# Feed-forward first products in three passes of split operands

## What is computed

```python
def ffn_layer(x, g, bln, W1, b1, W2, b2):
    mu = x.mean(-1, keepdims=True)
    var = ((x - mu) ** 2).mean(-1, keepdims=True)
    xn = (x - mu) / jnp.sqrt(var + 1e-05) * g + bln
    hg = xn @ W1 + b1
    a, gate = jnp.split(hg, 2, -1)
    return a * jax.nn.gelu(gate, approximate=False) @ W2 + b2
for i in range(DEPTH):            # 6 layers
    x = attn_layer(shift_tokens(x), Wqkv[i], q_scale[i], k_scale[i], Wo[i]) + x
    x = ffn_layer(shift_tokens(x), ln_g[i], ln_b[i], W1[i], b1[i], W2[i], b2[i]) + x
```

## Time and profile before

| | us |
|---|---|
| median of 3 runs | 2177.5 |
| lowest and highest run | 2176.08, 2187.78 |
| the profiled execution | 2168.39 |
| its span, first to last instruction | 2166.6 |

### The profile page before, as it was taken

How to read it: one execution, slowest core, us unless ns; L and a number is a source line. 1 busy time by engine, 2 the same in 40 slices (tenths; PEclk the granted TensorE clock), 3 DMA queues, 4 the chain that set the end, 5 groups by cost and what they waited for, 6 DMA issues and landing times.

```text
span 2166.6 us, 88603 instructions
## 1 busy us (share of the span) xinstructions
PE 1976.6 (91%) x37428; PEld 1424.8 (66%) x37428; DVE 1793.1 (83%) x3762; ACT 1633.8 (75%) x3052; POOL 1188.8 (55%) x1449
## 2 busy tenths in 40 slices
PE   6888899987789998999989999999999999899997
PEld 4666664455467776777767776677767777677774
DVE  6788775677789897898879988888888888888994
ACT  4777753365567897888888888888888888788883
POOL 1112110000477776766766768667776767767761
PEclk9999999998899998999999999999999999999999
DMA  5000011100122223232322323223233322333231
GB/s 115 2 2 2 2 31 46 43 1 26 41 64 75 62 76 90 66 81 68 79 77 68 79 66 103 68 59 87 60 90 78 79 68 69 88 76 83 59 79 41
DMA packets 98220, 132.57 MB, mean 61 GB/s; under 512 B 27900, under 2 KB 42882, under 8 KB 97826
## 3 DMA queue, kind: packets, MB, share of 16 engines
q1 hardware_dynamic: 97826, 126.90, 22.5%
HBM read 28.20 MB, written 1.11 MB: 14 GB/s over the span
## 4 chain that ended last, share of the span: by engine, by line
PE 65%; DVE 14%; ACT 9%; issue 8%; POOL 3%; SPq 0%; DMA 0%; DVEq 0%; POOLq 0%; ACTq 0%
PE oo L588 22%; PE pj L588 20%; PE sc L588 9%; PE tr L1011 7%; ACT arena L1886 7%; PE tr L591 4%; POOL arena L2316 2%; DVE arena L1462 1%; DVE arena L1707 1%; PE oo L591 1%; DVE xn L1294 1%; PE sc L591 1%; DVE arena L1705 1%; DVE arena L1736 1%; DVE arena L1713 1%
## 5 line engine op out<-in xcount | busy, mean ns | idle before, releaser
L1886 ACT ACTIVATE arena<-tr 128x512 f32<-128x512 f32 (+2 forms) x874 | 455.9, 568 | 135.4 <-PE tr L1011 67.7
L2298 POOL TENSOR_TENSOR arena<-arena 128x1024 f32<-128x1024 f32 x192 | 456.4, 2377 | 57.7 <-DVE arena L1707 54.1
L1886 ACT ACTIVATE arena<-arena 128x16 f32<-128x16 f32 (+6 forms) x808 | 356.0, 456 | 112.2 <-DVE arena L1462 74.1
L1886 ACT ACTIVATE arena<-pj 128x512 f32<-128x512 f32 x576 | 333.7, 597 | 86.1 <-PE pj L588 77.0
L2316 POOL TENSOR_TENSOR arena<-arena 128x1024 f32<-128x1024 f32 x192 | 365.5, 1904 | 27.5
L1705 DVE TENSOR_TENSOR arena<-pj,rtab 128x512 f32<-128x512 f32 x384 | 262.7, 684 | 59.1 <-ACT arena L1886 58.8
L1707 DVE TENSOR_TENSOR arena<-pj,rtab 128x512 f32<-128x512 f32 x384 | 261.4, 681 | 0.0
L1713 DVE TENSOR_REDUCE arena<-arena 128x8 f32<-128x512 f32 x384 | 251.8, 676 | 0.0
L588 PE MATMUL oo<-slab,arena 64*32 64x64 f32 (+1 forms) x12416 | 232.9, 229 | 10.2 <-issue 9.7
L2265 POOL TENSOR_SCALAR rstd<-mv 128x4 f32<-128x4 f32 x40 | 11.4, 284 | 400.6 <-DVE mv L1288 400.4
L591 PE MATMUL tr<-ident,arena 128*128 128x128 f32 x1346 | 207.0, 281 | 26.1 <-ACT arena L1886 12.1
(11 more groups left out here) (288 smaller groups left out, 3883.3 us busy)
## 6 DMA issues: line engine op xcount, KB each, us to landing
slab<-arena SPq DMA_DIRECT2D x576, 128.0 KB
slab<-arena SPq DMA_DIRECT2D x336, 64.0 KB
wqkv<-in_L_ffn_Wqkv SPq DMA_DIRECT2D x18, 512.0 KB, 3.6
arena<-gate_mem SPq DMA_DIRECT2D x24, 256.0 KB, 4.6
wo<-in_L_ffn_Wo SPq DMA_DIRECT2D x6, 512.0 KB, 4.8
w<-in_L_ffn_W SPq DMA_DIRECT2D x6, 341.0 KB
YT<-in_L_attn_x SPq DMA_DIRECT2D x4, 256.0 KB, 3.7
arena<-in_L_ffn_W SPq DMA_DIRECT2D x1, 1024.0 KB
```

The costliest lines, as they stand in the source:

```text
L1886: return nc.scalar.activation(o, i, f, **k)
L2298: p_.tensor_tensor(r_, r_, rb[:, k, :], ALU.add).then_inc(sum_ok, 1)
```

## The change

W1's columns and the normalized rows are split into a rounded copy and a rest, as the projections' operands are, and `ff_up` becomes six passes (three for each half) instead of two full products.

- ACT gains `up_high` (once a layer, in the slot b = 1, t = 3): `w1_hi`, the rounded copy of `w1`, 128 x 682. POOL gains `up_low` in the same slot, behind `add_parts(g, t, 1)`: the rest, written over `w1`.
- ACT gains `hidden_high` (once a batch, at t = 3 behind `ln_finish`): `hB_hi`, 128 x 512. POOL gains `hidden_low`, at t = 0 of the next slot, between `scaled` of the keys and `add_parts`: the rest, written over `hB`.
- TensorE waits for `w1_hi` and its rest at b = 2, t = 0, for `hB_hi` at t = 0, and for the rest of the rows before the third pass of the gate half.
- SP loads W1 in a function of its own (`up_weights`), ahead of the window copies of the slot b = 1, t = 3; it waits for the products of the layer before (`w1_mm`) instead of the second products.
- The gelu output has two buffers instead of three, which makes room for `w1_hi`; in the drain ACT waits for one `ff_gate` more.

```diff
+        w1_lo = nc.alloc_sbuf_tensor_at("w1_lo", [P, 2 * DI], F32R, offset=w1_at)
...
+        hB_hi = nc.alloc_sbuf_tensor_at("hB_hi", [P, S], F32R, offset=xcur_at + 4 * S)
...
+        hB_lo = nc.alloc_sbuf_tensor_at("hB_lo", [P, S], F32R, offset=hT_at)
...
-        ge = a.take(FFC, S)
+        ge = a.take(2, S)
+        w1_hi = nc.alloc_sbuf_tensor_at("w1_hi", [P, 2 * DI], F32R, offset=arena_at + 4 * a.at)
...
+            def up_weights(l):
+                wait(sp, w1_mm, l * B * FFC)
+                sp.dma_start(w1[:, :], ins["L1_ffn_W1"][l:l + 1].rearrange("a k n -> (a k) n")
+                             ).then_inc(ld_w1, 16)
...
+                if s_.later and b == 1 and t == 3:
+                    up_weights(l)
                 if s_.c_:
                     windows(g - 1, (t - 1) % T)
...
             def ff_up(m, k, bank):
-                o, w = CH[k]
-                mm(bank[0:w, 1], w1[:, DI + o:DI + o + w], hB)
-                mm(bank[0:w, 0], w1[:, o:o + w], hB).then_inc(w1_mm, 1)
+                w = CH[k][1]
+                for half, o in ((1, DI + CH[k][0]), (0, CH[k][0])):
+                    mm(bank[0:w, half], w1_hi[:, o:o + w], hB_hi[:, :], stop=False)
+                    mm(bank[0:w, half], w1_lo[:, o:o + w], hB_hi[:, :], start=False, stop=False)
+                    if half:
+                        pe.wait_ge(hb_l, m + 1)
+                    last = mm(bank[0:w, half], w1_hi[:, o:o + w], hB_lo[:, :], start=False)
+                last.then_inc(w1_mm, 1)
...
                     if b == 2 and t == 0:
-                        pe.wait_ge(ld_ff, s_.l2 * 64 + 64)
+                        pe.wait_ge(w1_l, s_.l2 + 1)
+                    if t == 0:
+                        pe.wait_ge(hb_h, m2 + 1)
                     pe.wait_ge(on_ok, g - 1)
                     ff_up(m2, t, oo)
...
+            def up_high(l):
+
+                ac.wait_ge(ld_w1, l * 16 + 16)
+                act(w1_hi[:, :], w1[:, :], ACT.Copy).then_inc(w1_h, 1)
+
+            def hidden_high(m):
+
+                ac.wait_ge(lnb_out, m + 1)
+                act(hB_hi[:, :], hB, ACT.Copy).then_inc(hb_h, 1)
...
                 if t == 3 and m1 is not None:
                     ln_finish(LNB, LNB_BANKS[1], m1, LC(m1, 0), LC(m1, 1), hB)
+                    hidden_high(m1)
...
                 ln_finish(LNB, LAST_NORM[1], MZ, LC(MZ, 0), LC(MZ, 1), hB)
+                hidden_high(MZ)
                 for k in range(FFC):
+                    if k == 2:
+                        ac.wait_ge(ff_ev, MZ * FFC + 1)
                     gelu(MZ, k, LAST_FF[MZ][k])
...
+            def up_low(l):
+
+                gp.wait_ge(w1_h, l + 1)
+                p_.tensor_tensor(w1_lo[:, :], w1[:, :], w1_hi[:, :], ALU.subtract).then_inc(w1_l, 1)
+
+            def hidden_low(m):
+
+                gp.wait_ge(hb_h, m + 1)
+                p_.tensor_tensor(hB_lo[:, :], hB, hB_hi[:, :], ALU.subtract).then_inc(hb_l, 1)
...
                     newton(g - 1, 1)
                     scaled(g - 1, (t - 1) % T, 1)
+                if t == 0 and s_.m2 is not None:
+                    hidden_low(s_.m2)
                 add_parts(g, t, 0)
...
                 add_parts(g, t, 1)
+                if b == 1 and t == 3:
+                    up_low(l)
...
             scaled(TZ, T - 1, 1)
+            hidden_low(MY)
             power(LNB, MZ)
+            hidden_low(MZ)
```

More of the change, by code:

```diff
@@ L160, in build @@
         wo = sb("wo", [P, PAIRS, P])
+        w1_at = here()
         w1 = sb("w1", [P, 2 * DI])
+        w1_lo = nc.alloc_sbuf_tensor_at("w1_lo", [P, 2 * DI], F32R, offset=w1_at)
         w2 = sb("w2", [P, FFC, P])
@@ L170, in build @@
         YT = sb("YT", [P, B * S])
+        xcur_at = here()
         xcur = sb("xcur", [P, 2, S])
+        hB_hi = nc.alloc_sbuf_tensor_at("hB_hi", [P, S], F32R, offset=xcur_at + 4 * S)
         hT_at = here()
         hT = sb("hT", [P, 2, S])
+        hB_lo = nc.alloc_sbuf_tensor_at("hB_lo", [P, S], F32R, offset=hT_at)
         xs_lo = nc.alloc_sbuf_tensor_at("xs_lo", [P, S], F32R, offset=hT_at + 4 * S)
@@ L190, in build @@
         ARENA = 27504
+        arena_at = here()
         arena = sb("arena", [P, ARENA])
@@ L285, in build @@
         oT = a.take(PAIRS, S)
-        ge = a.take(FFC, S)
+        ge = a.take(2, S)
+        w1_hi = nc.alloc_sbuf_tensor_at("w1_hi", [P, 2 * DI], F32R, offset=arena_at + 4 * a.at)
+        a.take(2 * DI)
         fa = a.take(FFC, S)
@@ L346, in build @@
             sem("pt_cp"), sem("o_mm"), sem("o_cp"), sem("wo_mm"), sem("y_att"), sem("xs_f"))
+        ld_w1, w1_h, w1_l, hb_h, hb_l = sem("ld_w1"), sem("w1_h"), sem("w1_l"), sem("hb_h"), sem("hb_l")
         w1_mm, gelu_ev, ff_ev, w2_mm, y_ff = (
@@ L500, in wo_weights @@
                              ).then_inc(ld_wo, 16)
+            def up_weights(l):
+                wait(sp, w1_mm, l * B * FFC)
+                sp.dma_start(w1[:, :], ins["L1_ffn_W1"][l:l + 1].rearrange("a k n -> (a k) n")
+                             ).then_inc(ld_w1, 16)
             def ff_weights(l):
                 wait(sp, w2_mm, l * B)
-                sp.dma_start(w1[:, :], ins["L1_ffn_W1"][l:l + 1].rearrange("a k n -> (a k) n")
-                             ).then_inc(ld_ff, 16)
                 for k, (o, n) in enumerate(CH):
@@ L562, in _ @@
             wo_weights(0)
+            up_weights(0)
             ff_weights(0)
@@ L1137, in ff_down @@
                     pe.wait_ge(ff_ev, m * FFC + 3)
+                    if b == 2:
+                        pe.wait_ge(ld_ff, s_.l2 * 48 + 48)
                     pe.wait_ge(t_sub, g - 1)
@@ L1228, in drain @@
                 pe.wait_ge(v_cp, TZ * 2 + 2)
-                pe.wait_ge(lnb_out, MY + 1)
+                pe.wait_ge(hb_h, MY + 1)
                 ff_up(MY, 0, LAST_FF[MY][0])
@@ L1264, in drain @@
                 norm_back(LNB, LAST_NORM[1], MZ)
-                pe.wait_ge(lnb_out, MZ + 1)
+                pe.wait_ge(hb_h, MZ + 1)
                 for k in range(FFC):
@@ L1761, in ff_gate @@
                 v.scalar_tensor_tensor(out=fa[0:w, k, :], in0=bank[0:w, 0], scalar=LC(m, 3 + k, w),
-                                       in1=ge[0:w, k, :], op0=ALU.add, op1=ALU.mult).then_inc(ff_ev, 1)
+                                       in1=ge[0:w, k % 2, :], op0=ALU.add, op1=ALU.mult).then_inc(ff_ev, 1)
             def slot(s_):
@@ L2131, in gelu @@
                 ac.wait_ge(w1_mm, m * FFC + k + 1)
-                act(ge[0:w, k, :], bank[0:w, 1], ACT.Gelu, bias=LC(m, 6 + k, w)).then_inc(gelu_ev, 1)
+                act(ge[0:w, k % 2, :], bank[0:w, 1], ACT.Gelu, bias=LC(m, 6 + k, w)).then_inc(gelu_ev, 1)
             def slot(s_):
@@ L2195, in slot @@
                     weights_high(l + 1, 0)
+                if b == 1 and t == 3:
+                    up_high(l)
                 if t == 0:
```

## The result

| | before | after | ratio |
|---|---|---|---|
| first measurement, median (us) | 2180.6 (2176.1 to 2187.8) | 2147.5 (2144.5 to 2155.1) | 0.9861 (95%: 0.9838 to 0.9883) |
| again, beside the experiments (us) | 2163.4 (2158.5 to 2168.8) | 2142.4 (2136.1 to 2145.0) | 0.9895 (0.9878 to 0.9913) |
| profiled execution (us) | 2168.39 | 2150.35 | |

The account below looks back on a forecast made before the run. TensorE bounds the slots with ff_up, ACT within 0.8 us. -21.1 (products) + 2 (stops) - 5.8 (boundary wait) - 3.4 (clock) + 3.7 (drain) = -24.6, from 2177.5 to 2152.9 us; own range 2141 to 2163, 8 in 10: 2141 to 2174.

Parts of the forecast that it names:

- The stretch: One ff_up on TensorE, first start to the window scores: six passes take 1.59 us instead of 1.91, saving 0.32.
- Products at the end: Feed-forward slots t = 0, 1, 2: 66 shorter ff_up stretches at 0.32 us each reach the end, -21.1 us.
- stops +2: TensorE's unexplained stops before window scores may grow where they follow ff_up: +2 us taken, between 0 and 7.4.
- ACT mostly stands ready and moves up too: ACT's gelu waited for PE's product 21.3 us in 35 cases, so ACT was expected to follow the shorter products.
- a slot of 14.5 still holds it, barely: At t = 2 ACT fills 14.0 of 14.8 us; the shortened slot was claimed still to hold that work.
- rival (2): Feed-forward slots: ACT takes over and only t = 0 gains, 7.0 us; total -10.5, 2167 us, chance 0.14.
- The splits: New copies on ACT and rests on POOL hide in idle time, cost 0; POOL's 2.8 us against 2.76 of idle.
- The boundary, A or B: Layer boundaries, behind hidden_low: A, DVE's waiting split goes next, -5.8 us; B, POOL's add goes first, +6.0, chance 0.22.
- The wait and the clock: Layer boundaries: value-weight split 1.16 us earlier in five layers, -5.8; less half-speed clock after PE's waits, -3.4, at most 13.6.
- the two short ones vanish: Of five half-clock spells after boundary waits, the two of 3.4 us disappear, giving -3.4 us.
- The drain: After the last slots: the third pass waits for hidden_low behind scaled, delaying the turn 3.4 us; in all +3.7.
- +0.6 and +0.3: Drain: +0.6 for the last batch's copy, split and slower passes; 0.3 us is a saving from one more stretch.

Follow-up runs that it names:

- the run with four: The changed kernel with ff_up in four passes instead of six, the products of rounded rows with the weights' rest left out: 2130.1 us, 0.9849.
- the run with the block put back: The changed kernel with hidden_low behind add_parts at b = 0, t = 0, so VectorE's value-weight split meets POOL's add again: 2153.2 us, 0.9927.
- the doubled run: The changed kernel with ScalarE's rounded copy of the rows made twice in all batches, POOL's rest in all but the boundary ones: 2150.1 us, 0.9936.
- the control: The changed kernel without further edits, measured again beside the experiments: 2142.4 us, 0.9895 of the kernel before.
- Order alone: The kernel before with one wait: at b = 0, t = 0 of layers 1 to 5 POOL starts add_parts after VectorE's value-weight split: 2147.2 us, 0.9908.

## Why the prediction was right

The sign and the size hold: forecast was a ratio of 2152.9 / 2177.5 = 0.9887, and 0.9861 and 0.9895 were measured. The main mechanism, shorter stretches that reach the end for the most part, held. That the sum came so near is in part luck: in the profiles the products off the boundaries gave 15 where 17.5 were forecast (61 x 0.32 less 2), the five boundary slots gave 14 to 15 where 10.8 were (5.8, 3.4 and their own 1.6 of products), and the drain took 4.5 where 3.7 were. (The upper end of the forecast's own range, 2163, should be 2165 by its own terms, -14.1 + 7.4 - 5.8 - 3.4 + 3.7 = -12.2; nothing hangs on it.)

- **The stretch** (1.59 forecast): 1.59. The steps are those of the projection. The old stretch of 1.91 us is eight times 0.239, and each of the two passes left out in the run with four took 0.23 (a stretch of 1.13 against 1.59). So the Trainium skill's count (FP8 and Floating Point Precision, TensorE Precision Notes: a true FP32 product is four passes) agrees with these numbers, other than the prediction said; the saving is a sixth and not a quarter because the first and the last step of the six take 0.34 and 0.32.
- **Products at the end** (-21.1, stops +2): some 14 by the run that undoes them, 16 and the drain's 4.5, so 20, by the run with the block put back, each give or take 6 or less, and 15 off the boundaries by the profiles. The step that failed is "ACT mostly stands ready and moves up too", with "a slot of 14.5 still holds it, barely". At the head of t = 1, 22 slots lose some 4 us to ACT, and behind the stretch of t = 2 they lose 2 to 3 (22 x 0.14 = 3 by the clean slots), so that rival (2) is a third true. Whether the stops grew by 2 can't be told: all of them in the feed-forward stage took 47 us before, and 51 and 41 in the two profiles after.
- **The splits** (hidden, 0): 0.63, 0.76, 1.29 and 1.65 us measured for 0.63, 0.84, 1.2 and 1.6, and hidden as far as the slots t = 3 and the doubled run show; the latter shows too that the cover has little left. The prediction's 2.8 us against 2.76 of idle never meet in one slot, since `hidden_low` stands at t = 0 and `up_low` at t = 3.
- **The boundary, A or B** (A): A in every one of the five layers, the split at 1.82 us where 1.7 was written. The order of two waiting engines was the open point, and the add of 3.36 us shows it: the engine that already stood waiting went in at the edge of POOL's instruction. That is in keeping with the lock that the Trainium skill describes (SBUF — State Buffer, Who interferes with whom).
- **The wait and the clock** (-5.8 and -3.4): the two were sized the wrong way round. The split did come 1.1 us earlier, but PE's idle time in those slots fell by 2.4 only, since PE then waits for `weighted`; the prediction named nothing that is late next. The clock gave 11, near its upper bound of 13.6. The failed step is "the two short ones vanish": all five did. Behind none of the five waits, now 0.7 us at most, did the granted clock fall; where it is below 1.00 in those slots (0.98 and 0.93) it had fallen before they began, at 816.5 and 1584.5. Not every wait costs the clock: in the same slots PE waits up to 1.16 us for ACT and 1.01 for `weighted`, and in this profile the clock fell behind none of these either. In the control's profile it fell once, behind the wait for `weighted` in layer 3. What sets one apart from another is open. Order alone, in the kernel before, has the clock ahead of the wait too: 10.4 and 6.5.
- **The drain** (+3.7): the last slot and the tail grew from 67.0 us to 71.5 in this profile and to 71.6 in the control, so +4.5. The wait of 3.77 us is the one that the prediction's times give (from 2118.4 to 2122.1). But the turn came 6.38 us behind the first pass instead of 1.83, so 4.5 later where 3.4 was written: the lower clock behind the wait, which the prediction left out, added the rest. Nothing is left over for its +0.6 and +0.3. Reordering takes the wait away.

Not settled: what moved the kernel before by 13 to 17 us between the two measurements, and with it the gain from 33 to 21. The order alone gives 20 us in the kernel before, where its five slots are 17 shorter, and its loss costs 7 in the changed one, where they are 13 to 14 longer; with uncertainties of 5 and 6, the first agrees with its slots and the second does so barely. In the changed kernel the slots t = 1 behind the boundaries are 2 to 3 us longer in sum than before, with as much more of stops for instructions.

## What to carry to other kernels

Price a wait on TensorE together with the clock that it costs afterwards: here 1.1 us of a wait, five times, gave back 11 us of PE's busy time. But look in the trace whether the clock does fall behind that wait, since other waits of about 1 us in the same slots cost nothing more. When a pass is made cheaper, look for the engine that is 0.1 us behind in each slot separately, and not in the shortest slots alone. Move a new producer ahead of work that nobody waits for yet. And before a rewrite is credited with a gain, try its side effect alone: one wait in the old kernel was worth nearly as much as the whole rewrite.

## What the runs showed of the hardware

Nearly all stops of TensorE that the profile calls "issue" follow the landing of a packet of its own instructions. One of 2.52 us, in the changed kernel, and the DMA queues in the same 4 us (1582 to 1586; packets, MB, share of 16 engines):

```profile
1585.77 0.53 PE L603 MATMUL sc<-arena 64*32 64x64 f32 x17 [2.52 <-issue]
```

```profile
DMA packets 466, 0.72 MB, mean 181 GB/s; under 512 B 120, under 2 KB 120, under 8 KB 465
...
q1 hardware_dynamic: 465, 0.71, 83.7%
q8 instruction: 1, 0.02, 2.1%
```

In these 4 us window copies held the 16 DMA engines to 84%, and to 79% in the stop itself (1583.25 to 1585.77). The one instruction packet of 16 KB among them landed at 1584.34, 1.43 us before PE went on. The granted clock fell to 0.50 in the middle of that stop and stayed there to 1591.3. More than nine in ten of all such stops, in each of the two profiles of the changed kernel and with thin copies, end 1.15 to 1.65 us behind the landing of such a packet, though only one lands in 7 us. That they bring TensorE's instructions is worked out: 299 packets, 4.90 MB, are 65 bytes for each of its 75144 products and weight loads, and all other engines together have 8300 instructions. The stops come mostly where instructions are short, 128 of them (64 products, 64 weight loads) in 0.9 us. So copies that TensorE was not seen to wait for can still hold it up, by way of its instructions: cutting the copies' bytes to an eighth, at the same number of transfers, took some 15 to 25 us of stops away, and the time fell by 23 us.
